# Moving the attention stage's row normalisation and the widening of its softmax sums from GpSimd to VectorE

## What is computed

```
def _L0_xattn_ref(v, k, q, mask, Wq, bq, Wk, bk, Wv, bv, Wo, bo):
    qh = _split_heads(q @ Wq + bq)
    kh = _split_heads(k @ Wk + bk)
    vh = _split_heads(v @ Wv + bv)
    logits = jnp.einsum('bhqd,bhkd->bhqk', qh, kh) / sqrt(DEPTH)
    logits = logits + mask * NEG_INF_SCALE
    attn = jax.nn.softmax(logits, axis=-1)
    out = jnp.einsum('bhqk,bhkd->bhqd', attn, vh)
    out = out.transpose(0, 2, 1, 3).reshape(B, Sq, D_MODEL)
    return out @ Wo + bo

x = x + mamba(_layernorm(x))
x = x + _L0_xattn_ref(ctx_1024, ctx_1024, _layernorm(x, axis=-1), mask, ...)
x = x + ffn(_layernorm(x))
```

## Time and profile before

| | us |
|---|---|
| median of 3 executions | 3492.78 |
| lowest and highest | 3491.26, 3498.7 |
| the profiled execution | 3491.26 |
| its span, first to last instruction | 3489.9 |
| busy in the span: PE, DVE | 3170.9 (91%), 2617.3 (75%) |
| busy in the span: ACT, POOL | 2392.2 (69%), 1900.4 (54%) |
| attention stage, from and to about | 1949, 3056 |

### The profile page before, as it was taken

How to read it: one execution, slowest core, us unless ns; L and a number is a source line. 1 busy time by engine, 2 the same in 40 slices (tenths; PEclk the granted TensorE clock), 3 DMA queues, 4 the chain that set the end, 5 groups by cost and what they waited for, 6 DMA issues and landing times. The chain is left out here.

```text
span 3489.9 us, 59895 instructions
## 1 busy us (share of the span) xinstructions
PE 3170.9 (91%) x20864; PEld 2214.2 (63%) x20864; DVE 2617.3 (75%) x4515; ACT 2392.2 (69%) x5339; POOL 1900.4 (54%) x1369
## 2 busy tenths in 40 slices
PE   5789889898889888988999799999999999999999
PEld 4566556665566556655665466666666666578887
DVE  2899999999999999999987576777677677523222
ACT  5777887878787887788774477777677777632222
POOL 2778887888787878788787111121121121055554
PEclk8899999999999999999999899999999999999999
DMA  5676665766667666666676121211121121120010
GB/s 164 158 189 184 183 167 161 203 188 164 154 193 192 164 165 179 184 175 155 171 193 185 62 71 47 79 62 47 61 79 47 53 83 65 48 73 25 33 41 25
DMA packets 286299, 425.04 MB, mean 122 GB/s; under 512 B 28753, under 2 KB 226129, under 8 KB 281394
## 3 DMA queue, kind: packets, MB, share of 16 engines
q1 hardware_dynamic: 278637, 411.44, 42.2%
q10 hardware_dynamic: 7365, 9.77, 0.9%
HBM read 320.12 MB, written 101.02 MB: 121 GB/s over the span
## 5 line engine op out<-in xcount | busy, mean ns | idle before, releaser
L811 POOL TENSOR_TENSOR a_hs<-a_rep,a_bmat 128x896 f32<-128x896 f32 x512 | 1061.2, 2096 | 287.1 <-PE a_yps L323 286.3
L443 ACT ACTIVATE a_states<-a_rep,a_a_neg 128x224 f32<-128x224 f32 x2048 | 793.5, 437 | 97.7 <-DVE a_hs L707 96.1
L700 DVE TENSOR_TENSOR_SCAN a_states<-a_states,a_hs 128x900 f32<-128x900 f32 x384 | 779.7, 2030 | 74.2 <-ACT a_states L443 59.2
L1414 DVE CUSTOM_DVE_ANT_0 b_sc<-sps,early_mask 112x375 f32<-112x375 f32 x1024 | 500.3, 545 | 182.4 <-PE sps L1171 173.6
L1311 ACT ACTIVATE b_sc<-b_sc,b_nmax 112x750 f32<-112x750 f32 x512 | 467.3, 913 | 10.4 <-DVE b_nmax L1420 10.4
L1185 PEld LDWEIGHTS b_tps<-ident,b_sc 112*125 112x125 f32 x3072 | 358.8, 190 | 150.3 <-issue 123.9
L345 PE MATMUL a_work<-early_scan_hT,w_in 128*128 128x224 f32 x2048 | 425.1, 363 | 6.9 <-issue 4.4
L707 DVE TENSOR_TENSOR a_hs<-a_states,a_cmat 128x896 f32<-128x896 f32 x384 | 419.2, 1092 | 13.2
L345 PEld LDWEIGHTS a_work<-early_scan_hT,w_in 128*128 128x128 f32 x2048 | 395.9, 196 | 47.8 <-issue 40.6
L1185 PE MATMUL b_tps<-ident,b_sc 112*125 112x112 f32 x3072 | 406.8, 282 | 9.3 <-DVE b_pT L1428 8.1
L1560 POOL COPY b_rwide<-b_rsum 112x128 f32<-112x128 f32 x128 | 33.7, 292 | 686.1 <-DVE b_rsum L1435 667.7
(11 more groups left out here) (199 smaller groups left out, 5030.3 us busy)
## 6 DMA issues: line engine op xcount, KB each, us to landing
a_rep<-du_scratch SPq DMA_DIRECT2D x512, 224.0 KB, 5.7
w_in<-W_in_dram SPq DMA_DIRECT2D x128, 512.0 KB, 4.3
du_scratch<-early_du SPq DMA_DIRECT2D x16, 1792.0 KB, 11.6
ctx<-ctxT_dram SPq DMA_DIRECT2D x48, 500.0 KB, 6.0
v_scratch<-kv_out SPq DMA_DIRECT2D x96, 250.0 KB
k_scratch<-kv_out SPq DMA_DIRECT2D x96, 250.0 KB, 4.5
b_keys<-k_scratch SPq DMA_DIRECT2D x8, 1500.0 KB, 8.7
b_v<-v_scratch SPq DMA_DIRECT2D x8, 1500.0 KB
```

The lines of the kernel that those rows point to most:

```text
L443: e = act.activation(rows(states[:, g % DA, :])[:, q, 1:ROW], rep[tile % REPS][:, j, 0, :], ACT.Exp, scale=a_neg[:, g % SLOTS, q:q + 1])
L700: dve.tensor_tensor_scan(state if g % G4 else whole, state, whole, 0.0, ALU.mult, ALU.add).then_inc(S["scan"], 1)
L811: pool.tensor_tensor(hs[g % RING][:, :, 1:ROW], rep[tile % REPS][:, j, 1, :].unsqueeze(1).broadcast_to([P, Q, L]), bmat[b % 2][:], ALU.mul ...
L1414: dve.tensor_tensor_reduce(out=sc[buffer_of(block)][:, j, cols], in0=sps[0:TT, j, 0:HALF], in1=mask[:, block % 2, cols], scale=-1.0, scala ...
```

## The change

GpSimd's function normalise becomes one of VectorE and is called in slot 11 (at = -5), ahead of keep_pT. It waits for the statistics and for early_rstd, which GpSimd still makes; add_bo stays on GpSimd and still waits for early_ln. GpSimd's widen_sums is gone: invert_sums now ends with the two copies into b_rwide on VectorE. Between the reciprocal and the copies VectorE waits for its own reciprocal to end (steps.settle). Before the reciprocal it waits for PE's spread_sums of the group before, where it had waited for GpSimd's widening of that group. The semaphore rsum is not needed any more. The calls of one slot stand in another loop, but in the same order.

```
@@ -1078,7 +1078,7 @@
             "xin0", "xin1", "xout0", "xout1", "stats1", "row_var", "row_log", "row_guess", "rstd",
             "ln", "res", "unit", "hT", "q32", "v0", "v1", "bv", "bo",
             "s_ps", "ttr", "nmax", "exp", "t_ps", "pt_act", "pt_dve",
-            "rsum", "rwide", "rb", "pv", "oT", "x2", "x2_read", "stats", "stats_out", "dve_step", "pool_step",
+            "rwide", "rb", "pv", "oT", "x2", "x2_read", "stats", "stats_out", "dve_step", "pool_step",
             "x2_var", "x2_log", "x2_guess", "x2_rstd", "biases", "const", "alpha2", "alpha2_row", "s1", "mv_in0", "mv_in1",
             "rows_in", "w2_in", "w2", "rows", "rows_hi", "rows_lo", "f_ps")
 
@@ -1393,6 +1393,16 @@
                     e = dve.bn_aggr(mv1[:, i, :], stats1[:, i, :])
                 e.then_inc(S["stats1"], 1)
 
+            def normalise(b):
+                dve.wait_ge(S["stats1"], b)
+                dve.wait_ge(S["rstd"], b)
+                if b >= 2:
+                    dve.wait_ge(S["unit"], unit_of["hT", b - 1, 1])
+                for i in range(2):
+                    e = dve.tensor_scalar(ln[:, i, :], xt[b % 2][:, i, :], mv1[:, i, 0:1], rstd[:, i:i + 1],
+                                          ALU.subtract, ALU.mult)
+                e.then_inc(S["ln"], 1)
+
             def widen_bv():
                 dve.wait_ge(S["bv_in"], 16)
                 dve.tensor_copy(bv_wide[:], bv[:].unsqueeze(2).broadcast_to([P, KD, TT])).then_inc(S["bv"], 1)
@@ -1431,8 +1441,12 @@
                 G = b * GROUPS + g
                 dve.wait_ge(S["exp"], 2 * GROUP * (G + 1))
                 if G:
-                    dve.wait_ge(S["rwide"], G)
-                dve.reciprocal(rsum[:], esum[:, :, g * GROUP:(g + 1) * GROUP]).then_inc(S["rsum"], 1)
+                    dve.wait_ge(S["unit"], unit_of["r", G - 1, 0])
+                steps.after(dve.reciprocal(rsum[:], esum[:, :, g * GROUP:(g + 1) * GROUP]))
+                steps.settle()
+                for i in range(2):
+                    e = dve.tensor_copy(rwide[:, i], rsum[:, i, :].unsqueeze(2).broadcast_to([TT, GROUP, DH]))
+                e.then_inc(S["rwide"], 1)
 
             def scale_o(b, g):
                 G = b * GROUPS + g
@@ -1510,12 +1524,12 @@
                     negate_and_mask(slot)
                 for b in range(B):
                     at = slot - b * SLOTS
+                    if at == -6 and b:
+                        stats_of_x1(b)
+                    if at == -5 and b:
+                        normalise(b)
                     if 6 <= at < 6 + SLOTS and (at - 6) % 4 == 0:
                         invert_sums(b, (at - 6) // 4)
-                for b in range(B):
-                    at = slot - b * SLOTS
-                    if at == -6 and b:
-                        stats_of_x1(b)
                     if at == SLOTS + 8:
                         row_stats(b)
                 if before:
@@ -1543,23 +1557,6 @@
                     pool.wait_ge(S["ln"], b - 1)
                 newton_rsqrt(steps, rstd[:], guess[:], var_eps[:], tmp[:]).then_inc(S["rstd"], 1)
 
-            def normalise(b):
-                pool.wait_ge(S["rstd"], b)
-                if b >= 2:
-                    pool.wait_ge(S["unit"], unit_of["hT", b - 1, 1])
-                for i in range(2):
-                    e = pool.tensor_scalar(ln[:, i, :], xt[b % 2][:, i, :], mv1[:, i, 0:1], rstd[:, i:i + 1],
-                                           ALU.subtract, ALU.mult)
-                e.then_inc(S["ln"], 1)
-
-            def widen_sums(G):
-                pool.wait_ge(S["rsum"], G + 1)
-                if G:
-                    pool.wait_ge(S["unit"], unit_of["r", G - 1, 0])
-                for i in range(2):
-                    e = pool.tensor_copy(rwide[:, i], rsum[:, i, :].unsqueeze(2).broadcast_to([TT, GROUP, DH]))
-                e.then_inc(S["rwide"], 1)
-
             def rsqrt_of_x2(b):
                 pool.wait_ge(S["stats"], b + 1)
                 if b:
@@ -1581,13 +1578,8 @@
             for slot in slots:
                 for b in range(B):
                     at = slot - b * SLOTS
-                    if 6 <= at < 6 + SLOTS and (at - 6) % 4 == 0:
-                        widen_sums(b * GROUPS + (at - 6) // 4)
-                for b in range(B):
-                    at = slot - b * SLOTS
                     if at == -6 and b:
                         rsqrt_of_rows(b)
-                        normalise(b)
                     if at == -6:
                         add_bo(b)
                     if at == SLOTS + 8:
```

## The result

The changed kernel takes 3510.3 us (median of 4 runs, 3506.99 to 3520.05) against 3493.24 for the kernel before in the same rounds: a ratio of 1.0052, 95% interval 1.0036 to 1.0067. It is 17.1 us slower. The forecast was 3499.3 with a range up to 3507: the direction was right, the size was not, and the difference lies in a rival that I had given too little.

The account below looks back on a forecast made before the run. PE was taken to bound the attention stage, waiting only behind DVE. The copies in slot 10 add 15 x 0.43 = 6.5 us, all else 0: 3492.8 + 6.5 = 3499.3 us, range 3494 to 3507.

Parts of the forecast that it names:

- What bounds the kernel: Attention stage: PE sets the pace, busy 957.5 of 1000 us, waiting behind DVE; nothing listed waits for POOL.
- Part 1: Two copies into b_rwide: slot 10 delays keep_pT by 0.43 us, 15 times, 6.5 us; other slots cost 0.
- Part 2: Normalisation on DVE in slot 11, about 1.0 to 1.05 us ahead of keep_pT, 15 times: cost 0.
- The margin of 0.1 us: Slot 12: spare time before PE would wait; normalising 0.3 us longer would make PE wait 0.2.
- Part 3: POOL loses 4 us of work; b_nmax in slot 11 returns to 0.16 us, freeing 0.44; gain 0 us.
- the sum: Whole kernel: 15 x 0.43 = 6.5 us from slot 10's copies, all else 0, median 3499.3 us.
- rival A: Waits in slots 10 and 11 halve PE's clock in one to four of 15: 3501 to 3506 us; chance 0.15.
- one wait of 1.63 us: Wait in the trace before, behind which PE's clock fell to 0.51 for about 3.5 us.
- one stretch: About 3.5 us of PE at half clock, doing the work of 1.75, so costing 1.7 us.
- Rival C: The 0.44 us freed behind b_nmax reaches PE; 6.6 us cancels the 6.5, 3492.7 us, no change; chance 0.13.

Follow-up runs that it names:

- Normalisation only: The changed kernel with invert_sums and widen_sums as before, so only normalise moves to VectorE, against the kernel before: 3490.29 us, ratio 0.9995.
- The kernel with PE filled in: The changed kernel with PE repeating four transposes in slot 10 and four in slot 11, against the kernel before: 3500.91 us, ratio 1.0022.
- the last version: Both moves of the change, with split statistics, widening and normalisation all behind keep_pT, against the kernel before: 3483.15 us, ratio 0.9977.
- the repeat: The changed kernel measured once more, nothing altered, against the kernel before: ratio 1.0055.
- widening only: Only b_rwide's widening moves to VectorE, normalise stays on GpSimd, against the kernel before: 3513.04 us, ratio 1.0054.

## Why the prediction was wrong

- What bounds the kernel, and that freeing GpSimd brings nothing: right. "Normalisation only" gives a ratio of 0.9995. The list does have one wait for GpSimd, where the prediction says that it has none: PE waits 3.0 us for GpSimd's c_gT_lo before its first matmul of the feed-forward stage. It is 3.0 in the changed kernel too.
- Part 1, the copies in slot 10: right in mechanism and size. I took 0.43 us; the wait grew from 0.54 to 0.97, and a sequence by 0.44. The groups of DVE in the changed kernel (busy us, mean ns) have 223 ns for a copy of 112x128, against my 225 from a line between two rows, and 165 for b_nmax. Slots 2, 6 and 14 were hidden, as were the last sequence's.

```profile
L1448 DVE COPY b_rwide<-b_rsum 112x128 f32<-112x128 f32 x128 | 23.2, 223 | 2.2
L1430 DVE TENSOR_TENSOR b_nmax<-b_half_min 112x4 f32<-112x4 f32 x128 | 21.1, 165 | 4.4
```

- Part 2, the normalisation: right. It took 1.00 us, rstd was there in time, and no wait arose in slot 12. The margin of 0.1 us was real: the kernel with the widening behind keep_pT used it up with masking 0.26 us later.
- Part 3: right. b_nmax takes 165 ns on average, where it took 0.60 in each slot 11, and nothing at the end follows from it. ACT's wait for it shrank from 10.4 us over 15 times to 2.5 over 9; the prediction had it gone.
- The step that failed is the sum: "15 x 0.43 = 6.5, all else 0", with the clock as rival A at a chance of 0.15, "one to four of 15". It was six, at about 1.6 us each: 6 x 1.6 = 9.6, and 6.6 + 9.6 = 16.2 of the stage's 17.0 us. The kernel with PE filled in shows that these 10 us are the clock's. My argument against it, "the idle time is in two pieces, with 1.5 us of work between", was no protection, and the piece of trace that I measured by, one wait of 1.63 us, was no measure of what the clock stands. Two pieces of 0.69 and 0.73 bring it down in six of 14 sequences, and one of 2.04, in the last version, didn't. I had priced one stretch rightly (1.7 us) and its frequency by feeling.
- The section of the Trainium skill that I had cited for this rival ("TensorE: Matmul & The Clock Gate", "A second HAM failure mode: psum-queue depth-cycling") tells of just such short idle times between groups of matmuls. With the waits of the kernel before the trace doesn't show it, with those of the changed one it does.
- Rival C, that the freed 0.44 us reach PE, is refuted by "normalisation only": 67.05 us.

Left open: which sequences become slow. The two waits are the same to 0.01 us in all of them, and in one execution the clock falls in six of 14. They don't look like separate chances, though. The 14 values of the changed kernel are 67.49, 69.10, 68.85, 67.50, 67.51, 69.10, 67.49, 69.10, 67.78, 69.09, 67.50, 69.07, 67.49, 69.06: from the sixth on every second one is slow. In the repeat the first, third, fifth, seventh and ninth are, and then the thirteenth. No run here shows what sets this order.

## What to carry to other kernels

- Before putting work on an engine that has 29% of idle time, look at what stands behind it in that slot. By the length of the stage, two small copies cost 17 us ahead of a copy that TensorE waits for, 3 us behind it with the normalisation still ahead of the next one, and nothing measurable once normalisation and statistics stood behind as well.
- Where TensorE has short waits that the clock just about stands, the price of a delay isn't its length: here 0.1 us more cost 1.5 us by the sequences and 0.19 us more cost 12. Count waits that lie close together as one (0.69 and 0.97 did what 0.24 and 0.98 didn't), and test a small dose before you trust a sum.
- Moving a piece of work forward to a place where nobody waits for it can bring it too close to the transfer that feeds it: look at who releases it there (once 1.97 us of wait here).
- Waits that a view lists at 0.5 us may be worth more (0.76 here); compare start to start with a place that has no wait.

## What was not expected of the hardware

That TensorE's clock falls behind two waits of 0.69 and 0.73 us with work between them, in six of 14 sequences, and not behind 0.24 and 0.98, nor behind a single one of 2.04 (above).

While GpSimd runs its first normalising instruction, a VectorE operation with two inputs in SBUF of 4 elements took 0.60 us instead of 0.16. The Trainium skill, "SBUF — State Buffer", section "SBUF: two separate sides", has a rule for this: the two engines share a port pair that one of them holds for a whole instruction. The block is there, but it ended 1.3 us before GpSimd's first of the two did (2067.70 against about 2069.0), so by this trace not the whole instruction is blocked. It ended 0.77 us after GpSimd's start; in "widening only", where b_nmax comes 0.42 us after GpSimd's start and not 0.17, it takes 0.36 us and ends 0.78 after it. Against another operation of GpSimd's the trace agrees with the rule: beside its addition of the bias, two of 112x512 from 1965.78 to 1968.28, b_nmax at 1967.87 ends at 1968.30. Times on GpSimd are rough in these profiles. Without the normalisation on GpSimd the 0.60 went.
